# Attention strips: the subtraction of the maxima on GpSimd, scores two iterations ahead in three buffers, row carry and stores on ScalarE

## The reference

```python
y = conv1x1(layer_norm(x), qkv_w, qkv_b)
win = unfold(y, 8, stride=6, pad=3)                 # windows of 64 pixels
attn = einsum("blhic,blhjc->blhij", q, k) + bias    # 64 x 64 for each window and head
e = exp(attn - max(attn, axis=-1))
s_img = fold(sum(e, axis=-1))                       # overlapping windows are added up
o_img = fold(einsum("blhij,blhjc->blhic", e, v))
out = conv1x1(o_img / s_img, proj_w, proj_b)
```

## Time and profile before

| | us |
|---|---|
| median of 3 runs | 5938.9 (5936.1 to 5944.1) |
| the profiled execution, its own time | 5927.0 |
| its span in the profile | 5925.2 |
| the stage of the attention strips in it | about 2564 to 3045 |

### The profile page before, as it was taken

How to read it: one execution, slowest core, us unless ns; L and a number is a source line. 1 busy time by engine, 2 the same in 40 slices (tenths; PEclk the granted TensorE clock), 3 DMA queues, 4 the chain that set the end, 5 groups by cost and what they waited for, 6 DMA issues and landing times. The chain is left out here.

```text
span 5925.2 us, 85841 instructions
## 1 busy us (share of the span) xinstructions
PE 5229.6 (88%) x34678; PEld 2383.1 (40%) x34678; DVE 4103.4 (69%) x4897; ACT 2823.1 (48%) x3955; POOL 811.0 (14%) x826
## 2 busy tenths in 40 slices
PE   7799999999979959978869799989878888888879
PEld 2355555555534424445534333333223333333323
DVE  3477767677611112268978499968879999999963
ACT  1144444444422212235531455526677777867744
POOL 1000000000000001122244100000033333323300
PEclk9899999999989979989989899989989999999999
DMA  6522122121031124344433101013310000000034
GB/s 215 134 38 41 24 39 42 21 41 23 15 90 66 58 52 154 111 140 145 132 123 133 45 23 34 31 45 105 102 41 17 16 28 15 26 28 5 16 111 163
DMA packets 313031, 398.46 MB, mean 67 GB/s; under 512 B 157484, under 2 KB 295461, under 8 KB 309373
## 3 DMA queue, kind: packets, MB, share of 16 engines
q1 hardware_dynamic: 280316, 303.11, 17.6%
q0 software_dynamic: 16096, 73.39, 3.6%
q10 hardware_dynamic: 16224, 16.48, 1.0%
HBM read 226.40 MB, written 166.50 MB: 66 GB/s over the span
## 5 line engine op out<-in xcount | busy, mean ns | idle before, releaser
L3899 DVE TENSOR_TENSOR_SCAN s_h<-s_da,s_h 128x448 f32<-128x448 f32 x672 | 730.0, 1125 | 1.6 <-ACT s_da L3826 1.5
L3746 PE MATMUL s_py<-s_prod,s_idf 128*128 128x448 f32 x1344 | 584.5, 557 | 24.7 <-ACT s_ycol L3839 23.4
L622 PE MATMUL b_pc<-b_ca,b_wdm 128*113 128x392 f32 x1152 | 487.1, 520 | 31.4 <-DVE b_wdm L837 25.5
L3826 ACT ACTIVATE s_da<-s_dt,s_al 128x448 f32<-128x448 f32 x672 | 405.8, 657 | 199.2 <-DVE s_h L3899 148.8
L765 ACT ACTIVATE b_band<-b_psel 124x784 f32<-124x784 f32 x264 | 217.7, 824 | 427.4 <-PE b_psel L690 424.3
L622 PE MATMUL b_pc<-b_cb,b_wdm 128*113 128x392 f32 x960 | 401.7, 518 | 0.0
L3884 DVE TENSOR_TENSOR s_h<-s_dtu,s_pb 128x896 f32<-128x896 f32 x336 | 355.3, 1058 | 28.5 <-POOL s_dtu L3933 22.5
L3906 DVE TENSOR_TENSOR s_prod<-s_h,s_pc 128x896 f32<-128x896 f32 x336 | 361.2, 1075 | 0.1
L3922 POOL TENSOR_TENSOR s_dt<-s_dt,s_dtu 128x448 f32<-128x448 f32 x168 | 249.3, 1484 | 782.6 <-DVE s_h L3899 422.6
L2851 DVE SCALAR_TENSOR_TENSOR j_zc<-j_zt,j_gw,j_zc 128x896 f32<-128x896 f32 x320 | 344.9, 1144 | 6.7 <-ACT j_zt L2790 6.4
L3746 PEld LDWEIGHTS s_py<-s_prod,s_idf 128*128 128x128 f32 x1344 | 248.7, 192 | 219.4 <-issue 166.5
(11 more groups left out here) (722 smaller groups left out, 11246.1 us busy)
## 6 DMA issues: line engine op xcount, KB each, us to landing
b_qk<-mid_qkvp SPq DMA_DIRECT2D x96, 240.2 KB
d_vt<-mid_vd SPq DMA_DIRECT2D x200, 96.0 KB
d_qs<-mid_qd SPq DMA_DIRECT2D x20, 744.0 KB, 5.6
d_ks<-mid_kd SPq DMA_DIRECT2D x20, 744.0 KB, 8.0
b_v<-mid_qkvp SPq DMA_DIRECT2D x6, 1922.0 KB
mid_pout<-d_out POOLq DMA_DIRECT2D x20, 558.0 KB, 4.4
mid_qkvp<-a_out SPq DMA_DIRECT2D x42, 248.0 KB, 2.3
mid_qkvp<-a_out ACTq DMA_DIRECT2D x42, 248.0 KB, 2.1
```

What stands on the lines that cost most here:

```text
L622: mm = pe.matmul(pc[n % 2][0:113, 0:392], wdm[:, slot, p, 0:113], src, start=(w == STARTS[a]), stop=(w + 1 == STARTS[a + 1]))
L3746: mm = pe.matmul(y, idf[:, :], prod[j % 3][:, e, :], start=(pr == 0 and e == 0), stop=False)
L3826: last = a.activation(da[j % 4][:, e, :], dt[s % 2][:, span(c)], ACT.Exp, scale=al[:, u, n:n + 1])
L3899: v.tensor_tensor_scan(x, along(da[j % 4][:, e, :]), x, before_, ALU.mult, ALU.add).then_inc(scanned, 1)
```

## The change

- The subtraction leaves soft and VectorE. GpSimd does it as shift(n), after the maxima of n; d_sc and d_mx get a third buffer.
- TensorE and VectorE take score and soft two iterations ahead instead of one.
- GpSimd's order becomes, for iteration n of strip s: shift(n), then one of the three window copies of strip s+1 (i = 0, 1, 2) or clear of s+1 (i = 3).
- carry moves to ScalarE as an activation (Copy), at i = 0 behind turn and expo and ahead of invert; store moves to ScalarE's queue, at i = 4 behind finish.

```diff
@@ -1909,8 +1909,8 @@
         ks = [sb(f"d_ks{i}", [128, 3, WS, PW]) for i in range(2)]
         qw = [sb(f"d_qw{i}", [128, 3, NR, 64]) for i in range(2)]
         vt = [sb(f"d_vt{i}", [128, 2 * C]) for i in range(NV)]
-        sc = [sb(f"d_sc{i}", [128, 2, 3 * 2 * 64]) for i in range(2)]
-        mx = [sb(f"d_mx{i}", [128, 12]) for i in range(2)]
+        sc = [sb(f"d_sc{i}", [128, 2, 3 * 2 * 64]) for i in range(3)]
+        mx = [sb(f"d_mx{i}", [128, 12]) for i in range(3)]
         et = [sb(f"d_et{i}", [128, 2, 3 * 128]) for i in range(2)]
         acc = [sb(f"d_acc{i}", [128, 6, WS, PW]) for i in range(2)]
         rec = sb("d_rec", [128, 3, ON])
@@ -1988,12 +1988,12 @@
 
         @block.gpsimd
         def _(p):
-            def window(s):
-                p.wait_ge(q_loaded[s % 2], 16 * (s // 2 + 1))
-                if s >= 2:
-                    p.wait_ge(scored, NP * (s - 1))
-                for t in range(3):
-                    p.tensor_copy(qw[s % 2][:, t, :, :].rearrange("p n (h w) -> p n h w", w=WS), windows(qs[s % 2][:, t, :])).then_inc(windowed, 1)
+            def window(s, t):
+                if t == 0:
+                    p.wait_ge(q_loaded[s % 2], 16 * (s // 2 + 1))
+                    if s >= 2:
+                        p.wait_ge(scored, NP * (s - 1))
+                p.tensor_copy(qw[s % 2][:, t, :, :].rearrange("p n (h w) -> p n h w", w=WS), windows(qs[s % 2][:, t, :])).then_inc(windowed, 1)
 
             def clear(s):
 
@@ -2002,29 +2002,21 @@
                 first = 2 if s % NR else 0
                 p.memset(acc[s % 2][:, :, first:, :], 0.0).then_inc(acc_zeroed, 1)
 
-            def carry(s):
-
-                p.wait_ge(laid, 2 * NP * s)
-                p.tensor_copy(acc[s % 2][:, :, 0:2, :], acc[(s - 1) % 2][:, :, STEP:WS, :]).then_inc(acc_ready, 1)
-
-            def store(s):
-                q, r = divmod(s, NR)
-                p.wait_ge(p_evac, 3 * (s + 1))
-                p.dma_start(rows(pout)[q, :, :, ON * r:ON * r + ON], out[s % 2][:, :, :]).then_inc(stored[s % 2], 16)
-
-            window(0)
+            def shift(n):
+                p.wait_ge(max_found, n + 1)
+                by = sc[n % 3][:, :, :].rearrange("p b (m j) -> p (b m) j", j=64)
+                p.tensor_tensor(by, by, mx[n % 3][:, :].rearrange("p (m o) -> p m o", o=1).broadcast_to([128, 12, 64]), ALU.subtract).then_inc(shifted, 1)
+
+            for t in range(3):
+                window(0, t)
             clear(0)
-            for s in range(NSTR):
-                if s + 1 < NSTR:
-                    window(s + 1)
+            for n in range(NW):
+                s, i = divmod(n, NP)
+                shift(n)
+                if s + 1 < NSTR and i < 3:
+                    window(s + 1, i)
+                if s + 1 < NSTR and i == 3:
                     clear(s + 1)
-                if s:
-                    store(s - 1)
-                if (s + 1) % NR:
-                    carry(s + 1)
-            store(NSTR - 1)
-            p.wait_ge(stored[0], 16 * NR)
-            p.wait_ge(stored[1], 16 * NR)
 
         @block.tensor
         def _(pe):
@@ -2054,7 +2046,7 @@
                     pe.wait_ge(et_evac, n)
                 for b in range(2):
                     for t in range(3):
-                        mm = pe.transpose(pT[:, b, 128 * t:128 * t + 128], sc[n % 2][:, b, 128 * t:128 * t + 128], idf[:, :])
+                        mm = pe.transpose(pT[:, b, 128 * t:128 * t + 128], sc[n % 3][:, b, 128 * t:128 * t + 128], idf[:, :])
                 mm.then_inc(turned, 1)
 
             def weigh(n):
@@ -2092,10 +2084,11 @@
                     pe.matmul(pP[hi, 0, 0:ON], wp[:, 2, 0:64], att[:, 2, :], start=False, stop=True).then_inc(projected, 1)
 
             score(0)
+            score(1)
             for n in range(NW):
                 s, i = divmod(n, NP)
-                if n + 1 < NW:
-                    score(n + 1)
+                if n + 2 < NW:
+                    score(n + 2)
                 turn(n)
                 if n:
                     weigh(n - 1)
@@ -2114,13 +2107,24 @@
 
             def expo(n):
                 a.wait_ge(shifted, n + 1)
-                a.activation(sc[n % 2][:, :, :], sc[n % 2][:, :, :], ACT.Exp).then_inc(exp_done, 1)
+                a.activation(sc[n % 3][:, :, :], sc[n % 3][:, :, :], ACT.Exp).then_inc(exp_done, 1)
 
             def turn(n):
                 a.wait_ge(turned, n + 1)
                 if n >= 2:
                     a.wait_ge(summed, n - 1)
                 a.activation(et[n % 2][:, :, :], pT[:, :, 0:384], ACT.Copy).then_inc(et_evac, 1)
+
+            def carry(s):
+
+                a.wait_ge(laid, 2 * NP * s)
+                a.wait_ge(acc_zeroed, s + 1)
+                a.activation(acc[s % 2][:, :, 0:2, :], acc[(s - 1) % 2][:, :, STEP:WS, :], ACT.Copy).then_inc(acc_ready, 1)
+
+            def store(s):
+                q, r = divmod(s, NR)
+                a.wait_ge(p_evac, 3 * (s + 1))
+                a.dma_start(rows(pout)[q, :, :, ON * r:ON * r + ON], out[s % 2][:, :, :]).then_inc(stored[s % 2], 16)
 
             def invert(s):
                 a.wait_ge(laid, 2 * NP * (s + 1))
@@ -2143,16 +2147,22 @@
                 if n + 1 < NW:
                     expo(n + 1)
                 if s and i == 0:
+                    if s % NR:
+                        carry(s)
                     invert(s - 1)
                 if s and i == 3:
                     finish(s - 1, 0)
                     finish(s - 1, 2)
                 if s and i == 4:
                     finish(s - 1, 1)
+                    store(s - 1)
             invert(NSTR - 1)
             finish(NSTR - 1, 0)
             finish(NSTR - 1, 2)
             finish(NSTR - 1, 1)
+            store(NSTR - 1)
+            a.wait_ge(stored[0], 16 * NR)
+            a.wait_ge(stored[1], 16 * NR)
 
         @block.vector
         def _(v):
@@ -2164,16 +2174,14 @@
             v.tensor_copy(wd[hi, hi], wp[hi, 1, 0:64]).then_inc(diag_ready, 1)
 
             def soft(n):
-                o = n % 2
+                o = n % 3
                 v.wait_ge(scored, n + 1)
-                if n >= 2:
-                    v.wait_ge(turned, n - 1)
+                if n >= 3:
+                    v.wait_ge(turned, n - 2)
                 v.tensor_tensor(sc[o][:, :, :], pS[:, :, 0:384], bt[:, :, :], ALU.add).then_inc(biased, 1)
                 v.wait_ge(biased, n + 1)
                 by = sc[o][:, :, :].rearrange("p b (m j) -> p (b m) j", j=64)
                 v.tensor_reduce(mx[o][:, :], by, AX.X, ALU.max).then_inc(max_found, 1)
-                v.wait_ge(max_found, n + 1)
-                v.tensor_tensor(by, by, mx[o][:, :].rearrange("p (m o) -> p m o", o=1).broadcast_to([128, 12, 64]), ALU.subtract).then_inc(shifted, 1)
 
             def lay(n):
                 s, i = divmod(n, NP)
@@ -2196,10 +2204,11 @@
                 v.tensor_tensor(att[:, :, :], acc[s % 2][:, 0:3, 0:STEP, :].rearrange("p t h w -> p t (h w)"), rec[:, :, :], ALU.mult).then_inc(divided, 1)
 
             soft(0)
+            soft(1)
             for n in range(NW):
                 s, i = divmod(n, NP)
-                if n + 1 < NW:
-                    soft(n + 1)
+                if n + 2 < NW:
+                    soft(n + 2)
                 if n:
                     lay(n - 1)
                 if s and i == 2:
```

## The result

The changed kernel takes 6049.3 us (median of 4 runs, 6043.4 to 6054.4) against 5940.7 (5936.1 to 5944.1): 1.0181 times as long, 95% interval 1.0165 to 1.0197. Forecast were 6083 and a range of 6035 to 6145. The profiled execution took 6049.1 us, its span 6047.3, 122.1 more than before. From the first q load of the strips to the first load of the next stage 597.3 us pass, where 483.2 passed before: 114.0 of the 122.1 lie in the strips. By the medians the change costs 108.7 us.

A forecast was written before the change was run, and what follows sets the result against it. VectorE (91% busy) was taken to bound the strips; after the change GpSimd's q wait would. Strips 1 to 18 add 18 x 8.35 = 150 us, strip 0 -1, strip 19 -4: +145, about 6083 us, range 6035 to 6145.

The forecast's parts named there:

- The step it rested on: GpSimd's queue: shift(5s+1) stands behind the window copy waiting for q, so can't start before T+8.0; strip 31.05 for 22.71 us.
- the signs that were named: In the strips: q issues 31 us apart, GpSimd waiting some 220 us for q, VectorE about 53%, subtractions 1.6 to 2.1 us.
- the forecast's own 6050 to 6105: Whole kernel: narrower range for load time, subtraction and part of the clock; the forecast had chance 0.68.
- strips 0 and 19: First and last attention strips, without the full wait: -1 us for strip 0, -4 for strip 19.
- the cheap subtraction: GpSimd's subtraction at 0.85 us: strip 6.35 us more, 109 in all, so 6047; cheaper chain, 6010 to 6045, chance 0.08.
- Clear as a second stop: GpSimd's clear(s+1) waits for divide(s-1) with shift(5s+4) behind it; clear 1.96 us, ending at T+22.1.
- T: End of weigh(5s-1) on TensorE, from which a strip's chain is counted; next T predicted 31.05 us later.
- Carry in the chain: carry on ScalarE, ahead of Ln and Exp, adds 0.85 us to each strip's chain; bounds 0.56 and 1.135.
- Stores and scores ahead: Store issues on ScalarE hidden with 0.6 us to spare; scores two ahead under 0.3 us a strip either way.
- Low clock: TensorE restarts at half clock after its wait: 1.3 us more a strip, 6106; extra by clock or subtraction, chance 0.17.
- Slow subtractions: GpSimd's subtractions take 3.2 us, strip 11.15 us more, so 6134; extra by clock or subtraction, chance 0.17.
- Faster, if the load isn't waited for: q is there at GpSimd's first copy, TensorE bounds the strip, 19.6 for 22.7 us: 5877; chance 0.05.

The follow-up runs named there:

- run 1: Changed kernel with SyncE issuing the q and k loads of strip s+2 at i = 3 of strip s; 5909.3 us, 0.9950 of the kernel before.
- run 3: Changed kernel with all three window copies at i = 2, loads where they were; 5952.6 us, 1.0024 of the kernel before.
- run 9: Changed kernel with each strip's q load issued as three thirds, each window copy waiting for its own; 6010.0 us, 1.0122 of the kernel before.
- run 7: Changed kernel with the subtraction back on VectorE, the rest of the change kept; 5940.7 us, 0.9983 of the kernel before.
- run 5: Changed kernel with three accumulators in place of two, so clear waits for an earlier strip's division; 6042.4 us, 1.0151 of the kernel before.
- run 6: Changed kernel with carry as a GpSimd copy ahead of the window copies, no longer on ScalarE; 6055.6 us, 1.0174 of the kernel before.
- run 11: Kernel of run 8 with the Exp of invert moved on ScalarE from i = 0 to i = 1; 5881.6 us, 0.9903 of the kernel before.
- run 8: Changed kernel with strip s+2's q load at i = 2, its k load at i = 3, and three accumulators; 5906.7 us, 0.9924 of the kernel before.
- run 2: Kernel before the change with the loads of strip s+2 issued at i = 4 of strip s; 5935.9 us, 0.9991 of the kernel before.

## Why the prediction was right

**The step it rested on** held: GpSimd stands before the first window copy of the next strip with the subtraction of 5s+1 behind it. Runs 1, 3 and 9 move, bypass and shorten that one wait, and the strip follows: by 7.8, by 4.9, and by 1.85 us for 1.89. Run 7 leaves the wait and takes away what stands behind it, and the loss is gone. Of the signs that were named, GpSimd's wait (some 220 us, measured 224.6) and VectorE's share (53%, measured 55%) came as forecast; the subtraction, at 1.47 us, lies below its 1.6 to 2.1.

**The sizes** were too large: 145 us were added up where the medians differ by 108.7, and 6049.3 falls just short of the forecast's own 6050 to 6105. It is the wide range that holds it. A strip was put 1.9 us too long at 31.05. Step by step, means over 17 strips of the changed kernel's timeline against the prediction's terms:

| part of a strip | predicted | measured |
|---|---|---|
| q issue to first copy | 6.0 | 5.24 |
| first copy to transposes of 5s+1 | 3.5 | 3.08 |
| to transposes of 5s+2 | 4.9 | 4.40 |
| to the next q issue | 16.65 | 16.41 |
| strip | 31.05 | 29.13 |

The load came sooner; the DMA queues were less full, 108 GB/s in the stretch against 140, which may be why, and wasn't tested. The subtraction took 1.47 us, where 1.85 was taken between 1.72 and 1.96; the lower reckoning, by the difference of two sizes, was nearer. By the GPSIMD Engine Reference of the Trainium skill (section 3.1) the estimate was 1.66; the measurement lies below that too. ScalarE's instructions overlap: the next begins 0.75 us after an exponential of 0.84 (2847.02 and 2847.77 above), which takes 0.1 off each link. The errors all point one way, and make 18 x 1.9 = 35 us. The sum of 145 stands against 114 in the strips: 18 x (29.13 - 22.71) = 115.6, and -1.6 for strips 0 and 19, where -5 was put down. Two slips changed nothing: the 6047 of the cheap subtraction adds up to 6048, and VectorE's 0.95 for the maxima stood in no row (the trace has 0.953).

**Clear as a second stop**: right in kind, nearly empty in size. The prediction let the exponential of 5s+4 end at T+24.9 and left out what TensorE does until then: from T+17.65 a score, transposes and weigh, project(.,0) and a score, an estimate of 0.86 + 1.85 + 2.2 + 0.86, to T+23.4. Measured, TensorE idles 0.72 us there, and run 5, which takes the stop away, has a strip 0.55 us shorter. **Carry in the chain**: the step that failed. It stands where it was said to, but was counted with its full 0.85 us; a parallel path of TensorE at the low clock is as long, and run 6 found it worth nothing (4.31 us for 4.40). **Stores and scores ahead**: hidden, as predicted (an issue took 0.37 us; run 7).

**The rivals.** *Low clock*: it came, with 0.50 granted from 2847 to 2853 us in the strip shown. The transposes of 5s+1 took 1.54 us in all 18 strips, where 0.87 is full clock, those of 5s+2 1.16 in the strip shown and 1.03 on average. It took the room that the prediction gave it and little more. As to the start after each wait this is what TensorE: Matmul & The Clock Gate of the Trainium skill says (section on HAM oscillation). *Slow subtractions*: refuted, 1.479 at most. *Faster, if the load isn't waited for*: 5877 was the price put on it, run 11 has 5882 and runs 1 and 8, with less removed, 5909 and 5907. Its mechanism is sound, but it wanted the earlier load, which the change didn't have, and to come near its price three accumulators and the split of invert as well.

## What to carry to other kernels

Before work is moved to an engine for its idle time, ask what it waits for while idle: behind an instruction that waits for a DMA, free time can't be used, and a wait that has cost nothing becomes part of the loop once the loop's own work is queued behind it. Look whether the awaited transfer is itself released by the loop; if so, the loop pays its full latency every round, and issuing it earlier can be worth more than shorter instructions: here 7.8 us a strip, against 0.55 us at most for the waits and instructions taken out by themselves in runs 5 and 6. Where two paths end together, shortening either alone shows nothing, which doesn't mean that neither counts.

## What the runs showed of the hardware

The 128x768 subtraction with a repeated operand on GpSimd took 1.467 to 1.479 us over the 100 instructions of the changed kernel, less than an addition of 128x672 with strided inputs in another stage (median 1.548), so the number of elements alone doesn't set it; which part the strides have wasn't tested. The same subtraction took 0.957 in the median on VectorE.

The window copies took 712 to 724 ns in all 60 cases of the changed kernel, 712 to 1813 before, and up to 1458 in run 7, with the subtraction back on VectorE. The changed kernel's row and then that of before:

```profile
L1996 POOL COPY d_qw<-d_qs x60: 712/718/724, 2571.2 to 3111.2; 128x640 f32<-128x640 f32 x60
```

```profile
L1996 POOL COPY d_qw<-d_qs x60: 712/722/1813, 2568.3 to 2995.8; 128x640 f32<-128x640 f32 x60
```

The Trainium skill's page SBUF — State Buffer (section on who interferes with whom) says that a VectorE instruction with two SBUF inputs and a GpSimd instruction that reads SBUF exclude each other. The runs agree. The copies are even in the changed kernel, and uneven in the three kernels that have the subtraction on VectorE (before, run 2, run 7): each slow one there overlaps such a subtraction, or twice the division, which reads two tiles of SBUF as well. Nor is the subtraction the only one: run 3 has it on GpSimd, and still two copies took 1.81 us and three GpSimd subtractions 2.55, each beside VectorE's division. Its three copies of one strip, 3.13 us in place of some 2.1, and the division:

```profile
2824.15 3.13 POOL L1996 COPY d_qw<-d_qs 128x640 f32<-128x640 f32 x3 [5.14 <-DMA d_qs<-mid_qd]
2825.29 1.41 DVE L2205 TENSOR_TENSOR d_att<-d_acc,d_rec 128x1116 f32<-128x1116 f32 x1
```
